# Second attention: maxima of block pairs from a difference and one block

## The chip, the cores and the metric

One core of one Trainium2 chip runs the kernel. The metric is device time in microseconds (us) of one execution, the median of the runs; lower is better. The engines are TensorE (PE), VectorE (DVE), ScalarE (ACT), GpSimd (POOL) and SyncE (SP), which here only issues transfers.

## What is computed

The reference is a network of two layers, each an attention and a feed-forward part with a layer norm behind each. The change is in the second attention, over 2048 tokens and 16 heads of 8 columns:

```python
G = -(j[None, None, None, :] - P[..., None]) ** 2 * 2.0 / Z[..., None] ** 2
scores = jnp.einsum('bhqd,bhkd->bhqk', q, k) / jnp.sqrt(jnp.float32(D))
scores = scores + G
probs = jax.nn.softmax(scores, axis=-1)
ctx = jnp.einsum('bhqk,bhkd->bhqd', probs, v)
ctx = ctx.transpose(0, 2, 1, 3).reshape(ctx.shape[0], key_len, H * D)
return ctx @ wo + bo
```

`P` and `Z` depend on the query and its head, `j` is the key's index. The softmax needs a maximum per query and head, or something near it, so that the exp doesn't overflow.

## The kernel before

The kernel runs four blocks of code one after the other: first attention, first feed-forward with the projections of the second attention, second attention with the last feed-forward. The change touches the last but one (a few transfers) and the last.

**Tiles and layout.** Queries and keys of a head lie as rows of bf16 parts: `qrows` and `krows` hold 60 rows per head (products of parts, and the rows that make up G), once in partitions 0 to 59 and once in 64 to 123. `krows` holds the first half of the keys in the lower copy and the second half in the upper one. Rows 60 and 61 of `qrows` take the negated maximum in two parts. A product over 60 or 62 rows uses half of TensorE's rows, so two that lie on different halves can run beside each other.

**Units.** A unit is one group of 4 heads (`HG`) with one chunk of 512 queries: 16 units (`NU`). Each has two kinds of work. The *blocks* find the maximum: for each head and each 128 queries, four products of 128 queries by 512 keys (`max_block`, L1757) into one of three PSUM banks of `ps_r`, each reduced over its keys by VectorE (L1899) into a column of `maxpart`. Block `b` has `k = b % 4`; `j = k % 2` is the half of the rows, and `c = k // 2` the chunk within it. That is 64 blocks a unit, 1024 in all. The *turns* do the attention itself: 8 turns a unit (`TU`), 128 in all, each with four heads. For one head TensorE makes two products of 128 keys by 512 queries into `ps_e` (`scores`, L1785), ScalarE takes the exp of both in one instruction (L1716), and TensorE multiplies the result with the values into `ps_o` (`pv`, L1795), for the turn before, in two halves of four heads.

**Order.** `plan()` writes it out. Before the first turn stand all 64 blocks of unit 0 and 8 of unit 1 (`BEFORE`), with four groups of small weight products among them (`weight_step`); ScalarE copies their results out. Then each turn carries 8 blocks, a unit and 8 blocks ahead (`blocks_of`), turns 0 to 118. The banks rotate: a block's product waits until the operation three places earlier in the order has been read out (`s_bf`). The PE loop of a turn:

```python
for hh in range(HG):
    scores(turn, hh)
    for op in rest[:1]:
        ring(op)
    if hh % 2 == late and turn > 0:
        pv(turn - 1, hh // 2)
    for op in rest[1:2]:
        ring(op)
    rest = rest[2:]
```

`late` is true in the second turn of a unit. `scores` waits until the exp of two heads before is done, `pv` until the exps of its turn are. Once a unit, VectorE makes the unit's maxima from `maxpart` (`split_max`, L1885 to L1891), TensorE transposes them (`mt`, L1769), VectorE copies them out (L1903), and SP sends them into rows 60 and 61 of `qrows` (`place_max`, L1638); the first `scores` of the next unit waits for that. Also once a unit, ScalarE copies `ps_o` out (L1723), TensorE transposes it (`fin`, L1774) and VectorE scales it (L1910, L1912). The last 9 turns have no blocks.

GpSimd adds a bias at the start of this part and then waits for the end. SP's queue loads the rows of the units ahead.

## Time and profile before

| | us |
|---|---|
| median of 3 runs (1779.0 to 1783.94) | 1779.66 |
| the profiled execution | 1781.96 |
| its span | 1780.2 |
| VectorE busy in the span | 1313.4 (74%) |
| TensorE busy (matmuls) | 1620.0 (91%) |
| ScalarE busy | 983.8 (55%) |
| GpSimd busy | 719.3 (40%) |
| reduces of blocks (L1899), 1024 | 634.4, 0.682 each |
| exps of the second attention (L1716), 512 | 504.8, 1.023 each |

The profile is of one execution. Busy times are sums of instruction spans; neighbours on one engine overlap by some 0.1 us, so a span is longer than the step from one to the next. In the timeline, rows merge neighbours of one kind: start, length of the whole row, engine, line, operation, out and in, count, and in brackets how long the engine had been idle before and what ended that. TensorE's granted clock (PEclk) is in parts of its full 2.4 GHz.

### The profile page before, as it was taken

The page shows a single profiled execution, that of the slowest core. Times are in us where ns is not written, and L with a number is a line of the kernel's source. Part 1 is how long each engine was busy: PE and PEld are TensorE (multiplying, and loading weights), DVE is VectorE, ACT ScalarE, POOL GpSimd, SP SyncE. Part 2 cuts the span into 40 slices and gives each one's busy share as a digit, 9 for nine tenths or more (in the row PEclk, how much of TensorE's full clock was granted, in tenths as well). Part 3 has the DMA queues.
Part 4 walks back from the last instruction along what each step waited for, and adds up shares of the span by engine and source line. Part 5 has one row for each costly group of instructions (what it writes and reads, how often), then busy time and mean ns, then how long its engine had stood idle before and what let it go on. Part 6 is the DMA issues. An engine that isn't in the chain of part 4 may idle for free. (4 is left out here: it accounts for less than half of the span.)

```text
span 1780.2 us, 28289 instructions
## 1 busy us (share of the span) xinstructions
PE 1620.0 (91%) x10680; PEld 477.6 (27%) x10680; DVE 1313.4 (74%) x2616; ACT 983.8 (55%) x1168; POOL 719.3 (40%) x462
## 2 busy tenths in 40 slices
PE   7899999999999999995988579999999999999995
PEld 3232333333332323222444211111111111111122
DVE  6767576666667575723555589999999999999964
ACT  2444545544545544442545306777777777777774
POOL 4577887878787878895222110000000000000012
PEclk8999999999999999996999758999999999999998
DMA  5100000000000000001012430111211121111000
GB/s 113 37 8 13 14 13 8 13 14 7 19 8 19 8 13 14 13 13 26 8 36 58 128 68 1 24 24 24 46 30 31 30 39 24 24 24 24 2 2 24
DMA packets 76217, 46.42 MB, mean 26 GB/s; under 512 B 22158, under 2 KB 74930, under 8 KB 76082
## 3 DMA queue, kind: packets, MB, share of 16 engines
q1 hardware_dynamic: 74738, 43.38, 11.4%
q8 instruction: 84, 1.38, 0.3%
q10 hardware_dynamic: 1344, 1.25, 0.2%
q14 instruction: 51, 0.42, 0.1%
HBM read 25.66 MB, written 9.31 MB: 20 GB/s over the span
## 5 line engine op out<-in xcount | busy, mean ns | idle before, releaser
L1899 DVE TENSOR_REDUCE maxpart<-ps_r 128x1 f32<-128x512 f32 x1024 | 634.4, 682 | 24.8 <-PE ps_r L1757 23.1
L1716 ACT ACTIVATE probs<-ps_e 128x1024 f32<-128x1024 f32 x512 | 504.8, 1023 | 193.1 <-PE ps_e L1785 187.9
L369 POOL TENSOR_TENSOR acc<-acc,probs 128x1024 f32<-128x1024 f32 (+3 forms) x256 | 503.2, 1965 | 77.6 <-ACT probs L422 56.1
L422 ACT ACTIVATE probs<-ps_e 128x1024 f32<-128x1024 f32 (+1 forms) x320 | 285.7, 901 | 371.0 <-PE ps_e L591 124.9
L1757 PE MATMUL ps_r<-krows,qrows 60*128 60x512 bf16 x1024 | 346.8, 402 | 50.5 <-DVE maxpart L1899 17.9
L608 PE MATMUL ps_o<-probs,v 128*64 128x512 f32 (+3 forms) x1280 | 307.6, 559 | 0.2 <-ACT pv_raw L429 0.2
L1681 POOL TENSOR_TENSOR rstd<-veps,power 128x4 f32<-128x4 f32 x8 | 8.1, 1012 | 698.5 <-DVE veps L1949 698.5
L698 DVE TENSOR_REDUCE maxpart<-ps_x 128x2 f32<-128x1024 f32 x192 | 234.5, 1221 | 74.7 <-PE ps_x L516 74.7
L1785 PE MATMUL ps_e<-qrows,krows 62*128 62x512 bf16 x1024 | 278.6, 386 | 2.3 <-ACT probs L1716 0.9
L1795 PE MATMUL ps_o<-probs,v 128*9 128x512 f32 x2048 | 269.5, 598 | 12.4 <-ACT probs L1716 12.3
L1757 PEld LDWEIGHTS ps_r<-krows,qrows 60*128 60x128 bf16 x1024 | 79.9, 94 | 468.2 <-DVE maxpart L1899 352.6
L701 DVE CUSTOM_DVE_ANT_0 masked<-ps_x,later 128x128 f32<-128x128 f32 (+3 forms) x256 | 114.9, 486 | 61.1 <-PE ps_x L516 60.0
L516 PE MATMUL ps_x<-k_hi,q_hi 64*128 64x512 f16 (+3 forms) x640 | 113.5, 351 | 21.0 <-DVE maxpart L698 17.3
L573 PE MATMUL ps_e<-q_hi,k_hi 64*128 64x512 f16 (+3 forms) x640 | 116.0, 359 | 0.4 <-ACT probs L422 0.3
L573 PE MATMUL ps_e<-q_lo,k_hi 64*128 64x512 f16 (+3 forms) x640 | 112.8, 349 | 0.0
L573 PE MATMUL ps_e<-q_hi,k_lo 64*128 64x512 f16 (+3 forms) x640 | 112.7, 349 | 0.0
L364 POOL TENSOR_TENSOR acc<-probs 128x1024 f32<-128x1024 f32 x32 | 75.2, 2351 | 79.6 <-ACT probs L422 79.6
L608 PEld LDWEIGHTS ps_o<-probs,v 128*64 128x64 f32 x1280 | 63.7, 135 | 87.0 <-issue 76.2
L780 DVE TENSOR_TENSOR ps_e<-ps_e,ahead 128x256 f32<-128x256 f32 (+1 forms) x128 | 55.5, 443 | 25.6 <-PE ps_e L573 16.2
L573 PEld LDWEIGHTS ps_e<-q_hi,k_hi 64*128 64x128 f16 x640 | 30.8, 93 | 159.1 <-issue 106.1
L1785 PEld LDWEIGHTS ps_e<-qrows,krows 62*128 62x128 bf16 x1024 | 58.6, 94 | 30.2 <-ACT probs L1716 11.8
L591 PE MATMUL ps_e<-mrow,negone 2*128 2x512 bf16 (+3 forms) x640 | 60.2, 356 | 0.0
(305 smaller groups left out, 1396.1 us busy)
## 6 DMA issues: line engine op xcount, KB each, us to landing
qrows<-q_rows SPq DMA_DIRECT2D x64, 192.0 KB
rbc<-rden SPq DMA_DIRECT2D x128, 64.0 KB, 2.1
q_rows<-parts_q SPq DMA_DIRECT2D x24, 128.0 KB, 2.3
k_rows<-parts_k SPq DMA_DIRECT2D x24, 128.0 KB, 2.3
krows<-k_rows SPq DMA_DIRECT2D x16, 192.0 KB, 5.4
w_rows<-parts_w SPq DMA_DIRECT2D x6, 256.0 KB, 2.6
qrows<-a_rows SPq DMA_DIRECT2D x64, 24.0 KB
qrows<-w_rows SPq DMA_DIRECT2D x64, 24.0 KB
```

Of the source, the lines that this page charges most:

```text
L369: pool.tensor_tensor(acc[:, u % 2, :, o:], acc[:, u % 2, :, o:], probs[:, turn % RING, :, o:], ALU.add)\
L422: act.activation(probs[:, turn % RING, :, o:], ps_e[:, turn % 2, :, o:], ACT.Exp, scale=1.0 / math.sqrt(D0))\
L516: mm = pe.matmul(ps_x[:, h, 0:w], hi["q"][rows, p % 2, (4 * qc + t) * P:(4 * qc + t + 1) * P], hi["k"][rows, p % 2, c * QC:c * QC + w], st ...
L573: mm = pe.matmul(out[:, h, o:], k_part["k"][rows, p % 2, keys], q_part["q"][rows, p % 2, queries], start=n == 0 and turn % 2 == 0, stop=n ...
L608: mm = pe.matmul(ps_o[D0 * h:D0 * h + D0, o:], v[:, p % 2, kt, D0 * h:D0 * h + D0], probs[:, turn % RING, h, o:], start=kt == 0, stop=kt = ...
L698: dve.reduce_max(maxpart[:, u % 2, :, t, c:c + 1], ps_x[:, :, 0:w], AX.X).then_inc(s_xf, 1)
L701: ins = dve.tensor_tensor_reduce(out=masked[:, h, 0:w], in0=ps_x[:, h, 0:w], in1=later[:, QC - w:QC], scale=1.0, scalar=-3e38, op0=ALU.add ...
L1716: act.activation(probs[:, HG * (turn % 2) + hh], ps_e[:, e % 2], ACT.Exp).then_inc(s_ex, 1)
L1757: return pe.matmul(out, qrows[64 * j:64 * j + R_M, u % 3, c, hh, t * P:(t + 1) * P], krows[64 * j:64 * j + R_M, u // NQ % 2, hh, c * KB:(c ...
L1785: mm = pe.matmul(ps_e[:, e % 2, j], krows[64 * j:64 * j + R_END, u // NQ % 2, hh, at * P:(at + 1) * P], qrows[64 * j:64 * j + R_END, u % 3 ...
L1795: mm = pe.matmul(ps_o[32 * hh:32 * hh + D1 + 1, :], v1[:, TU * j + at, HG * (u // NQ) + hh, :], probs[:, HG * (turn % 2) + hh, j, :], star ...
L1899: dve.reduce_max(maxpart[:, at:at + 1], ps_r[:, k, :], AX.X).then_inc(s_bf[k], 1)
```

## The change

For a pair of blocks `b` (even) and `b+1`, which have the same queries and the keys of the two halves, one product over 124 rows gives the difference of the two: its left side is both copies of the query rows, its right side the keys of the first block above and the *negated* keys of the second below (`nrows`). ScalarE takes the Relu of it (`over`). VectorE reads block `b+1` from its bank, adds `over` and takes the maximum in one instruction: the sum of `s1` and `relu(s0 - s1)` is the larger of the two. The first block isn't computed for itself. `DIFF` lists the pairs: in unit 0 and the 8 blocks ahead all but the first four pairs (32 pairs), then one pair in four, the first of each turn (119). In a turn the order of the 8 blocks becomes 0, 2, 3, 1, 4, 5, 6, 7.

`nrows` is filled by ScalarE (its negated half) and GpSimd (the copied half) for the first group, by GpSimd for the others. Rows 60 to 63 of `nrows` and `qrows` are set to zero by 8 transfers from `zrow`. `maxpart` is set to -3e38 first, so that the columns of the left-out blocks don't matter; PE waits for that memset too.

```diff
@@ stage before, SP @@
-            sp.wait_ge(s_cr, 5)
+            sp.wait_ge(s_cr, 6)
+            for row in range(R_M, 64):
+                sp.dma_start(qrows[row:row + 1].rearrange("a u c h (x n) -> a (u c h x) n", n=KB),
+                             zrow[0:1, :, :].to_broadcast([1, 3 * 2 * HG, KB])).then_inc(s_z, 16)
@@ stage before, DVE @@
+            dve.memset(zrow[0:1, :, :], 0.0).then_inc(s_cr, 1)
...
@@ blocks_of @@
-            return [("max", b) for b in range(first, min(first + LEAD, NU * BU))]
+            return [("max", first + n) for n in (0, 2, 3, 1, 4, 5, 6, 7) if first < NU * BU]
...
+        DIFF = {b: n for n, b in enumerate([b for b in range(2 * NC, BU + LEAD) if b % 2 == 0] +
+                                           [b for b in range(BU + LEAD, NU * BU) if b % (2 * NC) == 0])}
+        DIFF_OF = {b + 1: n for b, n in DIFF.items()}
+        RING_OF = {op[1]: op[2:] for op in ALL if op[0] == "max"}
+        JOINS = sorted(DIFF_OF)
@@ SP @@
+            for row in range(R_M, 64):
+                sp.dma_start(nrows[row:row + 1].rearrange("a b h (c n) -> a (b h c) n", n=KB),
+                             zrow[0:1, :, :].to_broadcast([1, 2 * HG * HALF // KB, KB])).then_inc(s_z, 16)
@@ POOL @@
+            def negate_k(g):
+                pool.wait_ge(s_k[g % 2], 16 * NQ * (g // 2 + 1))
+                rows = slice(64, 64 + R_M)
+                pool.tensor_scalar(nrows[rows, g % 2], krows[rows, g % 2], -1.0, None, ALU.mult).then_inc(s_neg, 1)
+                pool.wait_ge(s_neg, g + 1)
+
+            def copy_k(g):
+                pool.wait_ge(s_k[g % 2], 16 * NQ * (g // 2 + 1))
+                pool.tensor_copy(nrows[0:R_M, g % 2], krows[0:R_M, g % 2]).then_inc(s_cpy, 1)
+                pool.wait_ge(s_cpy, g + 1)
+
+            copy_k(0)
...
+            for g in range(1, NG):
+                negate_k(g)
+                copy_k(g)
@@ ACT @@
+            def positive(b):
+                n, (k, m) = DIFF[b], RING_OF[b]
+                act.wait_ge(s_bp[k], m + 1)
+                if n >= 2:
+                    k1, m1 = RING_OF[JOINS[n - 2]]
+                    act.wait_ge(s_bf[k1], m1 + 1)
+                act.activation(over[:, n % 2, :], ps_r[:, k, :], ACT.Relu).then_inc(s_bf[k], 1)
...
+            act.wait_ge(s_k[0], 16 * NQ)
+            rows = slice(64, 64 + R_M)
+            act.activation(nrows[rows, 0], krows[rows, 0], ACT.Copy, scale=-1.0).then_inc(s_neg, 1)
+            for n, op in enumerate(BEFORE):
+                if op[0] == "max" and op[1] in DIFF:
+                    positive(op[1])
+                if n in (8, 16, 24, 32):
+                    weights_out(n // 8 - 1)
             for turn in range(NU * TU):
                 u, at = divmod(turn, TU)
                 for hh in range(HG):
                     exps(HG * turn + hh)
+                    for op in TURNS[turn][2 * hh:2 * hh + 2]:
+                        if op[0] == "max" and op[1] in DIFF:
+                            positive(op[1])
@@ PE, max_block @@
+                if b in DIFF:
...
+                    return pe.matmul(out, qrows[0:64 + R_M, u % 3, c, hh, t * P:(t + 1) * P],
+                                     nrows[0:64 + R_M, u // NQ % 2, hh, c * KB:(c + 1) * KB], start=True, stop=True)
...
-            pe.wait_ge(s_cv, 2)
+            pe.wait_ge(s_cv, 3)
@@ DVE @@
             dve.memset(ps_o[:, :], 0.0).then_inc(s_cv, 1)
+            dve.memset(maxpart[:, :], -3e38).then_inc(s_cv, 1)
             dve.tensor_copy(identb[:, :], ident[:, :]).then_inc(s_cv, 1)
...
+                if kind == "max" and i in DIFF:
+                    return
                 dve.wait_ge(s_bp[k], m + 1)
-                if kind == "max":
+                if kind == "max" and i in DIFF_OF:
+                    at, n = i % (2 * BU), DIFF_OF[i]
...
+                    dve.tensor_tensor_reduce(out=larger[:, n % 2, :], in0=ps_r[:, k, :], in1=over[:, n % 2, :], scale=1.0, scalar=-3e38,
+                                             op0=ALU.add, op1=ALU.max, accum_out=maxpart[:, at:at + 1]).then_inc(s_bf[k], 1)
+                elif kind == "max":
```

What moves on TensorE in a steady turn. Before, from the block ahead of the first `pv` to the second `pv`, each row with the semaphore it waits for (`s_bf10` to `s_bf12` are the three banks of `ps_r`):

```order
L1757 MATMUL ps_r<-krows,qrows 128x512 [waits s_bf11]
L1795 MATMUL ps_o<-probs,v 9x512 [waits s_ex1]
L1795 MATMUL ps_o<-probs,v 9x512 x3
L1757 MATMUL ps_r<-krows,qrows 128x512 [waits s_bf12]
L1785 MATMUL ps_e<-qrows,krows 128x512 [waits s_ex1]
L1785 MATMUL ps_e<-qrows,krows 128x512
L1757 MATMUL ps_r<-krows,qrows 128x512 [waits s_bf10]
L1757 MATMUL ps_r<-krows,qrows 128x512 [waits s_bf11]
L1785 MATMUL ps_e<-qrows,krows 128x512 [waits s_ex1]
L1785 MATMUL ps_e<-qrows,krows 128x512
L1757 MATMUL ps_r<-krows,qrows 128x512 [waits s_bf12]
L1795 MATMUL ps_o<-probs,v 9x512 [waits s_ex1]
```

And with the change (L1823 is the product of the difference, L1825 a block, L1853 the scores, L1863 `pv`; the bank numbers are those of another turn, only their rotation matters):

```order
L1863 MATMUL ps_o<-probs,v 9x512 x3
L1825 MATMUL ps_r<-krows,qrows 128x512 [waits s_bf11]
L1853 MATMUL ps_e<-qrows,krows 128x512 [waits s_ex1]
L1853 MATMUL ps_e<-qrows,krows 128x512
L1825 MATMUL ps_r<-krows,qrows 128x512 [waits s_bf12]
L1825 MATMUL ps_r<-krows,qrows 128x512 [waits s_bf10]
L1853 MATMUL ps_e<-qrows,krows 128x512 [waits s_ex1]
L1853 MATMUL ps_e<-qrows,krows 128x512
L1825 MATMUL ps_r<-krows,qrows 128x512 [waits s_bf11]
L1863 MATMUL ps_o<-probs,v 9x512 [waits s_ex1]
L1863 MATMUL ps_o<-probs,v 9x512 x3
L1825 MATMUL ps_r<-krows,qrows 128x512 [waits s_bf12]
```

The product ahead of the first `pv` is now the difference. The block behind it still waits for one bank, and the block ahead of the second `pv` for the same bank again, as before.

What moves on ScalarE at the start of this part. Before, after the weight copies, it loads its table and starts on the exps:

```order
L1734 ACTIVATE w_t<-ps_e 128x128
L1734 ACTIVATE ua_t<-ps_e 50x128
L1734 ACTIVATE lu_t<-ps_e 4x50
L1734 ACTIVATE ld_t<-ps_e 100x4
L1737 ACTIVATE inner<-ps_e 4x128
L1737 ACTIVATE outer<-ps_e 50x128
L1737 ACTIVATE w_d<-ps_e 128x128
L1716 ACT_TABLE_LOAD
L1716 ACTIVATE probs<-ps_e 128x1024 x36
```

With the change, from behind the first four weight copies on (ahead of these rows stand the negation of the keys, one Relu and those four copies); L1774 is the Relu, L1785 a weight copy, L1753 the exp:

```order
L1774 ACTIVATE over<-ps_r 128x512 x4
L1785 ACTIVATE inner<-ps_e 4x128
L1774 ACTIVATE over<-ps_r 128x512 x4
L1785 ACTIVATE outer<-ps_e 50x128
L1774 ACTIVATE over<-ps_r 128x512 x4
L1785 ACTIVATE w_d<-ps_e 128x128
L1774 ACTIVATE over<-ps_r 128x512 x19
L1753 ACT_TABLE_LOAD
L1753 ACTIVATE probs<-ps_e 128x1024
L1774 ACTIVATE over<-ps_r 128x512
L1753 ACTIVATE probs<-ps_e 128x1024 x4
L1774 ACTIVATE over<-ps_r 128x512
```

The table load and the first exp now stand behind 32 Relus, and each turn's four exps have one Relu among them.

## Rows read from the trace of the kernel before

**Rows 1.** Windows: per stretch each engine's busy time (instructions), then PEclk, DMA share, GB/s.

```profile
1031.60:1071.00 39.40, 38.22 (x75) 7.50 (x75) 38.28 (x64) 2.82 (x8) 4.90 (x5) 0.50 0.27 50
1076.00:1084.50 8.50, 8.50 (x34) 1.42 (x34) 7.86 (x14) 6.14 (x6) 0.00 (x0) 0.50 0.01 2
...
1172.67:1215.25 42.58, 39.72 (x263) 7.93 (x261) 40.77 (x71) 31.94 (x33) 0.00 (x0) 1.00 0.12 25
```

**Rows 2.** Timeline of one steady turn, from PV1 to the next PV1.

```profile
1188.70 1.05 PE L1795 MATMUL ps_o<-probs,v 128*9 128x512 f32 x8 [0.16 <-ACT probs L1716]
...
1189.68 0.39 PE L1757 MATMUL ps_r<-krows,qrows 60*128 60x512 bf16 x1
1189.68 0.60 PE L1785 MATMUL ps_e<-qrows,krows 62*128 62x512 bf16 x2
...
1190.10 4.95 DVE L1899 TENSOR_REDUCE maxpart<-ps_r 128x1 f32<-128x512 f32 x8 [0.21 <-PE ps_r L1757]
...
1190.32 1.94 ACT L1716 ACTIVATE probs<-ps_e 128x1024 f32<-128x1024 f32 x2 [0.76 <-PE ps_e L1785]
...
1190.85 0.39 PE L1757 MATMUL ps_r<-krows,qrows 60*128 60x512 bf16 x1
...
1191.17 1.04 PE L1795 MATMUL ps_o<-probs,v 128*9 128x512 f32 x8
...
1192.79 1.94 ACT L1716 ACTIVATE probs<-ps_e 128x1024 f32<-128x1024 f32 x2 [0.53 <-PE ps_e L1785]
...
1193.86 1.05 PE L1795 MATMUL ps_o<-probs,v 128*9 128x512 f32 x8 [0.16 <-ACT probs L1716]
```

**Rows 3.** Timeline of DVE in the first attention; last row from the groups by shape.

```profile
768.53 0.69 DVE L701 CUSTOM_DVE_ANT_0 masked<-ps_x,later 128x512 f32<-128x512 f32 x1 [1.08 <-PE ps_x L516]
769.15 0.08 DVE L701 DVE_READ_ACCUMULATOR2_ANT maxpart<- 128x1 f32 x1
769.15 0.69 DVE L701 CUSTOM_DVE_ANT_0 masked<-ps_x,later 128x512 f32<-128x512 f32 x1
...
L1723 ACT ACTIVATE pv_raw<-ps_o 128x512 f32<-128x512 f32 x16 | 9.5, 592 | 2.0 <-PE ps_o L1795 2.0
```

**Rows 4.** Timeline around the end of a unit: PV1 of four turns, and the maximum's way.

```profile
1172.67 1.04 PE L1795 MATMUL ps_o<-probs,v 128*9 128x512 f32 x8
...
1199.03 1.05 PE L1795 MATMUL ps_o<-probs,v 128*9 128x512 f32 x8 [0.16 <-ACT probs L1716]
...
1201.60 0.20 DVE L1903 COPY maxrow<-ps_r 64x128 bf16<-64x128 bf16 x1
...
1204.61 0.39 PE L1785 MATMUL ps_e<-qrows,krows 62*128 62x512 bf16 x2
...
1205.14 1.04 PE L1795 MATMUL ps_o<-probs,v 128*9 128x512 f32 x8
...
1215.25 1.05 PE L1795 MATMUL ps_o<-probs,v 128*9 128x512 f32 x8
```

**Rows 5.** Timeline: a GpSimd cast in the stage before, then the first unit.

```profile
1002.90 0.61 POOL L1071 CAST parts_q<-qs 128x512 bf16<-128x512 f32 x1 [7.97 <-DVE qs L1413]
...
1031.66 1.01 PE L1757 MATMUL ps_r<-krows,qrows 60*128 60x512 bf16 x3 [17.28 <-DMA qrows<-w_rows]
...
1032.28 4.28 DVE L1899 TENSOR_REDUCE maxpart<-ps_r 128x1 f32<-128x512 f32 x7 [0.96 <-PE ps_r L1757]
...
1041.83 0.59 PE L1810 MATMUL ps_e<-end_da,ld_t 100*4 100x128 f32 x2
...
1052.40 1.28 ACT L1716 ACT_TABLE_LOAD   x1
...
1072.14 0.29 PE L1769 MATMUL ps_r<-identb,maxhl 128*64 128x128 bf16 x1 [1.38 <-DVE maxhl L1891]
...
1075.91 0.66 PE L1785 MATMUL ps_e<-qrows,krows 62*128 62x512 bf16 x2
...
1076.61 1.02 ACT L1716 ACTIVATE probs<-ps_e 128x1024 f32<-128x1024 f32 x1 [22.93 <-PE ps_e L1785]
```

More of the change, by code:

```diff
@@ L823, in build @@
     qrows = l1.enter_context(nc.sbuf_tensor("qrows", [P, 3, 2, HG, QC], BF16))
+    zrow = l1.enter_context(nc.sbuf_tensor("zrow", [1, 1, KB], BF16))
+    s_z = l1.enter_context(nc.semaphore("s_z"))
     s_q = [l1.enter_context(nc.semaphore(f"s_q{b}")) for b in range(3)]
@@ L1523, in build @@
         rowmax = sb("rowmax1", [P, HG * 4], F32)
+        nrows = sb("nrows", [P, 2, HG, HALF], BF16)
+        over = sb("over", [P, 2, QC], F32)
+        larger = sb("larger", [P, 2, QC], BF16)
         maxhl = sb("maxhl1", [P, 2, 2, HG * 4], BF16)
@@ L1552, in build @@
         s_bf = [sem(f"s_bf1{k}") for k in range(3)]
+        s_neg = sem("s_neg1")
+        s_cpy = sem("s_cpy1")
         s_rm = sem("s_rm1")
@@ L1729, in copy_step, with weights_out @@
                                ACT.Copy).then_inc(s_bf[k], 1)
-            for n, (dst, rows, cols) in enumerate(((w_t, P, DM), (ua_t, UD, P), (lu_t, RANK, UD), (ld_t, DD, RANK))):
-                act.wait_ge(s_lp, n + 1)
-                act.activation(dst[:, :], ps_e[0:rows, n // 2, n % 2, 0:cols], ACT.Copy).then_inc(s_lc, 1)
-            for n, (dst, rows) in enumerate(((inner, RANK), (outer, UD), (w_d, P))):
+            def positive(b):
[5 more added lines that the diff above has]
+                act.activation(over[:, n % 2, :], ps_r[:, k, :], ACT.Relu).then_inc(s_bf[k], 1)
+            def weights_out(step):
+                if step == 0:
+                    for n, (dst, rows, cols) in enumerate(((w_t, P, DM), (ua_t, UD, P), (lu_t, RANK, UD), (ld_t, DD, RANK))):
+                        act.wait_ge(s_lp, n + 1)
+                        act.activation(dst[:, :], ps_e[0:rows, n // 2, n % 2, 0:cols], ACT.Copy).then_inc(s_lc, 1)
+                    return
+                n = step - 1
+                dst, rows = ((inner, RANK), (outer, UD), (w_d, P))[n]
                 act.wait_ge(s_lp, 5 + n)
                 act.activation(dst[:, :], ps_e[0:rows, n // 2, n % 2, P:2 * P], ACT.Copy).then_inc(s_lc, 1)
+            act.wait_ge(s_k[0], 16 * NQ)
[6 more added lines that the diff above has]
+                    weights_out(n // 8 - 1)
             for turn in range(NU * TU):
@@ L1756, in max_block @@
                     pe.wait_ge(s_k[u // NQ % 2], 16 * NQ * (u // NQ // 2 + 1))
+                if b in DIFF:
+                    if b == 2 * NC:
+                        pe.wait_ge(s_z, 16 * 2 * (64 - R_M))
+                    if b == 2 * NC or b % (NQ * BU) == 0:
+                        pe.wait_ge(s_neg, u // NQ + 1)
+                        pe.wait_ge(s_cpy, u // NQ + 1)
+                    return pe.matmul(out, qrows[0:64 + R_M, u % 3, c, hh, t * P:(t + 1) * P],
+                                     nrows[0:64 + R_M, u // NQ % 2, hh, c * KB:(c + 1) * KB], start=True, stop=True)
                 return pe.matmul(out, qrows[64 * j:64 * j + R_M, u % 3, c, hh, t * P:(t + 1) * P],
@@ L1968, in normalize @@
                     ins.then_inc(s_no, 1)
+            dve.wait_ge(s_cv, 3)
             done = 0
```

10 lines of the change are left out of this document (9 added, 1 removed).

## The prediction

> **What bounds the kernel now.** I read the views in this order. The windows [rows 1] first: the first unit of the second attention (64 blocks, 1032 to 1071 us) runs with VectorE busy nearly all the time and TensorE's granted clock at 0.50 (the 1.2 GHz level), and a later unit takes 42.58 us with VectorE busy for 40.77 of them and ScalarE for 31.94. By shares, VectorE looks like the bound. The timeline of one turn [rows 2] says otherwise. I call the block products M0 to M7, the score products S, the first and second half of the probs-times-v products PV1 and PV2. From PV1 at 1188.70 the chain is: M1 starts 0.98 later (1189.68), VectorE starts its reduce 0.42 after that (1190.10), M4 needs the bank which that reduce empties and starts 0.75 later (1190.85), PV2 0.32 later (1191.17), then the last head's S and its exp, whose start is 1.62 after PV2 (1192.79), and the next PV1 waits for that exp: 1.07 (1193.86). The sum is 5.16, which is the distance of the two PV1. VectorE's eight reduces (4.95) lie beside it, with 0.21 idle. So one reduce is on the chain, the seven others are not: a steady turn is a loop of latencies through three engines, only 0.21 longer than VectorE's own work.
>
> **The change in the steady turn.** Per turn it removes one reduce on VectorE and gives ScalarE a Relu of 128x512. The joined maximum is a two-input operation with an accumulator; the same one in the first attention took 0.69, the read of its accumulator lay beside the next operation, and the next one started 0.62 after it [rows 3]. Reduces start (4.95-0.68)/7 = 0.61 apart [rows 2]. So the join costs what one reduce costs, and VectorE falls from 4.95 to about 4.33 a turn. The Relu has no row; the copy of the same shape took 0.592 [rows 3], half an exp's step would be 0.46. I take 0.59. It comes after the turn's first exp, where ScalarE sat idle 0.76 [rows 2], so it fits and no exp moves.
>
> What I look for is whether the loop above loses a link. It doesn't. The order of the blocks is now D0 (the difference), M2, M3, B1 (the partner), M4. With three banks in rotation M4 needs the bank of M2, the product right behind PV1, as it needed that of M1 before. The links 0.98, 0.42, 0.75, 0.32, 1.62, 1.07 all stay, and the turn stays at 5.16. VectorE only idles more, 0.83 instead of 0.21.
>
> D0 is new work on TensorE: it fills all the rows, so it can't run beside a score product on the other half, as M0 did. A half-height product takes one slot of 0.215 (two S in 0.60, one alone 0.39 [rows 2]). VectorE takes M2 1.40 after PV1 (0.98+0.42), then M3, B1, M4 and M5 at 0.615 each, so M5 starts at 3.87, D0's bank is free 0.75 later, at 4.62, and the next PV1 stands at 5.16: it may take 0.54 up to PV1. From M4 to PV2, which is also a product and a change of tile form, took 0.32 [rows 2]. I take 0.32 for D0, 0.42 if a change ahead of it costs the same 0.1 as the one behind it. Both are under 0.54, so in a steady turn it costs nothing; its cover is the wait for the exp. The Trainium skill ("TensorEngine Tiling (Array Packing)", Key Properties) says that changing the tiling mode drains TensorE. By it every D0 has a drain on both sides; by the row alone one drain of 0.1 stands in the 0.32. The sum is the same either way until the two together pass 0.54.
>
> **Turns that are not steady**, once a unit. (a) The last turn: its first PV1 to the next unit's is 6.11 instead of 5.16 [rows 4], since the transposed maximum is copied at 1201.60 behind two reduces, and the next unit's S waits for the transfer until 1204.61, 3.01 later. One of the reduces in front is gone (M0's), so copy and transfer come 0.55 earlier, and S at 5.03 after PV1 instead of 5.58. Late next is D0's bank: PV2 at 2.55, M4's reduce at 3.95, M5's at 4.57, D0 at 5.32, PV1 at 5.68 with 0.36 for D0. Gain 0.43. (b) From the first to the third turn, 10.11 [rows 4]. PV1 and PV2 of the second turn come one head later, so in the third there is no exp to wait for, and D0's slot and drain (0.32) stand in the open: 10.43, loss 0.32. (c) From 1172.67 to 1199.03 are five turns, 26.36; four steady ones leave 5.72 for the one that transposes the context; the reordered blocks move nothing there that I can see. Net gain 0.1 a unit, 1.5 for 15 units; bounds -7 and +7 (half a us a unit either way, the size of (a) and (b)).
>
> **The first unit.** Eight plain blocks as before, so D8 starts near 1032.28 + 5x0.60 + 0.73 = 1036.0, plus 0.1 for the extra memset that the products wait for [rows 5]. The negated and copied keys must be there: 4096 elements are 3.7 us on ScalarE at an exp's rate (0.92 per 1024, [rows 2]) and 4.9 on GpSimd at that of the cast of 512 in 0.61 [rows 5]; started at about 1030.6 they end by 1035.5. The eight extra transfers of zeros are on SP's queue ahead of loads needed 35 us later, and in the stage before ahead of ones waited for much later: nothing. GpSimd's bias adds move back by 5 us and are waited for at the end only; its six later passes over the keys lie in idle time.
>
> Then pairs. At half clock a product takes 0.43, twice the slot, and I add 0.1 for each change between half and full height: D and B together 1.06. The other loop is D, 0.62 to the Relu (as 1031.66 to 1032.28, [rows 5]), 0.59, 0.04, join 0.69, 0.05 to the product after next: 2.0 for two pairs. So 1.06 per pair, TensorE now the bound, against 1.20 for two reduces. 28 pairs are 29.7; the four groups of weight products (0.59 for one [rows 5], put at 0.6 each) had been beside VectorE's work and are now on the path: 2.4. D64 starts at 1068.2, the transposed maximum 1.9 later (join, three small operations) at 1070.1, against 1072.14: gain 2.0. The first exp was at 1076.61; its table load of 1.28 lay in idle time and now stands behind the last Relu [rows 5]: D70 near 1073.0, +0.62 +0.59 +1.28 = 1075.5, gain 1.1, with 0.3 won back in the first turn: 1.4. Bounds: 6 lost if a pair takes 1.3, 5 more gained if it takes 0.90.
>
> **Sum.** 1.4 + 1.5 = 2.9. Against the profiled execution (span 1780.2, time 1781.96, so 1.8 around it): span 1777.3, time 1779.1. That execution is 2.3 above the median of the three runs, 1779.66; against the median I forecast 1776.7. A measurement of this kernel can tell about 0.3%, 5.3 us, from no change, so this is no difference.
>
> **Rivals.** (A) Faster: the clock rises in the first unit. TensorE's rows show 0.50 both while one product ran per 0.60 and in the first turn with four per 1.20 [rows 1], rising only after the first PV. Pairs put a full-height product into each 1.06, more work than the first unit had but no more than that turn had. If it rises after a quarter of the pairs, a pair takes 0.90 (the 2.0 loop with products at full clock): 24x0.16 = 3.8, and about 2 from the first turns: 1771. The rows of the first turn speak against, the fuller engine for: 0.2. The Trainium skill ("TensorE: Matmul & The Clock Gate", What's actually happening) has the array throttled by default and activity release it; by that rule a fuller engine may rise, and the first turn's rows agree with it only in part.
> (B) Much faster: VectorE was the bound after all, and a turn gets shorter by the reduce that left. The busy share speaks for it, the chain of [rows 2] against. The floor then is that chain without the bank wait: M4 four slots behind M2, 0.98+4x0.215 = 1.84 after PV1 instead of 2.15, so 4.85; 119 turns x 0.31 = 37, less 3 more: 1740. Chance 0.07.
> (C) Slower: D0 delays PV1. It decides at 0.54 from D0's start to PV1. If weight load and drains ahead of and behind a full-height product come to 0.3 to 0.5 more than its slot, each turn is longer by 0 to 0.18; at 0.15 it is 119x0.15 = 18, less 3: 1795. For it: it is one change of form more per turn, and no row shows such a product there. Against: the 0.32 measured. Chance 0.15. The drains of the page on tiling are this mechanism.
> (D) The first unit's pairs take 1.3 or more: (1.3-1.06)x32 = 8, less 3: 1784. Chance 0.05.
>
> **Numbers.** Forecast 0.53, own range 1772 to 1781. Faster by over 0.3%: A 0.2, B 0.07, and 0.08 of the forecast where the units gain more: 0.35. Slower: C 0.15, D 0.04: 0.19. The rest, 0.46, within. The range 1767 to 1787 takes in A, the forecast, D and the mild end of C.
>
> **What would show it.** Right: PV1 to PV1 5.16 in steady turns with VectorE idle 0.8; Relu about 0.59 and join 0.69; 6.1 becoming 5.7 at a unit's end, 10.1 becoming 10.4; pairs 1.06 apart at clock 0.50; the first exp near 1075.5. Wrong: a steady turn of other than 5.16 (below: B, above with D0 just ahead of PV1: C), or the clock above 0.50 before 1070 (A).

## The result and the profile after

| | us | ratio to the kernel before, 95% interval |
|---|---|---|
| before, median of 20 runs | 1780.68 | |
| after, median of 20 runs | 1784.81 | 1.0023 [1.0014, 1.0032] |
| after, the profiled execution | 1782.89 | |
| its span | 1780.9 | |

The change makes the kernel 4.1 us slower, 0.23%. The forecast was a gain of 2.9. The time lies in the stated range (1767 to 1787) but outside the forecast's own (1772 to 1781), and the change is below the 5.3 us that the prediction took as the limit of one measurement; with 20 runs of each it is told from nothing all the same, and its sign is the other one.

Of the turns the profile says what was forecast. Groups of instructions (line, engine, operation, count, then busy us and mean ns, then idle time before and what ended it); reduces of the same shape were 1024 before:

```profile
L1979 DVE TENSOR_REDUCE maxpart<-ps_r 128x1 f32<-128x512 f32 x722 | 460.1, 684 | 85.5 <-PE ps_r L1825 85.5
...
L1975 DVE CUSTOM_DVE_ANT_0 larger<-ps_r,over 128x512 bf16<-128x512 f32 x151 | 103.2, 684 | 23.8 <-PE ps_r L1825 23.3
...
L1774 ACT ACTIVATE over<-ps_r 128x512 f32<-128x512 f32 x151 | 90.7, 601 | 22.4 <-PE ps_r L1823 22.4
```

151 joins and 151 Relus stand in place of 302 reduces. VectorE is busy for 1231.7 us instead of 1313.4, ScalarE for 1061.5 instead of 983.8. A steady turn from its timeline, one turn ahead of the one in [rows 2]:

```profile
1181.52 0.39 PE L1823 MATMUL ps_r<-nrows,qrows 124*128 124x512 bf16 x1
1182.07 1.04 PE L1863 MATMUL ps_o<-probs,v 128*9 128x512 f32 x8 [0.16 <-ACT probs L1753]
1182.81 0.60 ACT L1774 ACTIVATE over<-ps_r 128x512 f32<-128x512 f32 x1
...
1183.47 1.29 DVE L1979 TENSOR_REDUCE maxpart<-ps_r 128x1 f32<-128x512 f32 x2 [0.81 <-PE ps_r L1825]
...
1184.22 0.39 PE L1825 MATMUL ps_r<-krows,qrows 60*128 60x512 bf16 x1
1184.53 1.05 PE L1863 MATMUL ps_o<-probs,v 128*9 128x512 f32 x8
1184.68 0.68 DVE L1975 CUSTOM_DVE_ANT_0 larger<-ps_r,over 128x512 bf16<-128x512 f32 x1
...
1186.68 0.39 PE L1823 MATMUL ps_r<-nrows,qrows 124*128 124x512 bf16 x1
1187.23 0.62 PE L1863 MATMUL ps_o<-probs,v 128*9 128x512 f32 x4 [0.16 <-ACT probs L1753]
```

PV1 to PV1 is 1187.23 - 1182.07 = 5.16, as before. VectorE starts its first reduce 1.40 after PV1 and has been idle 0.81 by then, not 0.21. The difference product D0 starts 0.55 ahead of the next PV1, and PV1 is released by the exp, not by D0. VectorE gave up 0.6 a turn and nothing moved: it was not the bound.

What did move stands at the entry of the second attention. The executions reach it at different times (1030.7 in the profile of before, 1027.9 in that of after; in the executions of the experiments from 1027.3 to 1034.2), so from here on I align the traces at VectorE's first memset of this stage. The entry after:

```profile
1027.71 3.61 ACT L1789 ACTIVATE nrows<-krows 60x4096 bf16<-60x4096 bf16 x1 [8.58 <-PEq L862]
1027.71 3.59 POOL L1691 COPY nrows<-krows 60x4096 bf16<-60x4096 bf16 x1 [23.84 <-POOLq L862]
1027.88 0.48 DVE L1943 MEMSET ps_o<- 128x512 f32 x1 [7.23 <-PEq L862]
1028.38 0.17 DVE L1944 MEMSET maxpart<- 128x128 f32 x1
1028.46 2.93 DVE L1945 CAST identb<-ident 128x128 bf16<-128x128 f32 x1
...
1031.44 1.03 PE L1825 MATMUL ps_r<-krows,qrows 60*128 60x512 bf16 x3 [20.03 <-DVE identb L1945]
```

and before, where the first product came 0.95 after the memset [rows 5]:

```profile
1030.71 0.48 DVE L1875 MEMSET ps_o<- 128x512 f32 x1 [7.09 <-PEq L860]
1031.11 0.21 DVE L1876 CAST identb<-ident 128x128 bf16<-128x128 f32 x1
```

The cast of the identity matrix takes 2.93 instead of 0.21. It ends at 1031.39, 0.09 after GpSimd's copy of the keys has ended (1027.71 + 3.59), and TensorE's first product waits for it: 3.56 after the memset instead of 0.95, so 2.6 are lost. None of the tiles that these three operations write is read by that product: `ps_o` is first used by `pv`, `identb` by `mt`, `maxpart` by VectorE itself. The wait asks for more than the product needs; whether moving it to the first use would do as well as the experiments below was not run.

The Trainium skill ("SBUF — State Buffer", Who interferes with whom) says that GpSimd has no port of its own into this memory but VectorE's second pair, that a VectorE copy or cast can take both pairs, and that the one which comes second is then blocked for the whole instruction of the other. The two numbers, 2.93 and 0.09, agree with it.

Behind that, the first unit ran at the forecast pace (windows, columns as in [rows 1], then its timeline):

```profile
1032.00:1071.00 39.00, 37.35 (x78) 7.95 (x75) 25.39 (x69) 18.48 (x36) 19.08 (x7) 0.50 0.29 49
```

```profile
1066.01 0.61 PE L1823 MATMUL ps_r<-nrows,qrows 124*128 124x512 bf16 x1
...
1067.09 0.61 PE L1823 MATMUL ps_r<-nrows,qrows 124*128 124x512 bf16 x1
...
1074.18 1.28 ACT L1753 ACT_TABLE_LOAD   x1
...
1075.47 1.02 ACT L1753 ACTIVATE probs<-ps_e 128x1024 f32<-128x1024 f32 x1
```

A pair takes 1.08 and the granted clock stays at 0.50, though TensorE is busy for 37.35 of 39.00 us (whole spans count, 0.61 for one product), now in part with full-height products.

The third piece is in the units. I took the start of every PV1 and PV2 in both traces. Per unit there are 16 distances, and 12 of them are the same to 0.02. The other four, as means over 14 units:

| distance (the D0 or the blocks of that place) | before | after | forecast |
|---|---|---|---|
| PV2 to PV1, issued in the third turn (D0 in the open) | 1.52 | 1.84 | +0.32 |
| PV1 to PV2, in the same turn (the context's transposition between) | 2.64 | 2.85 | 0 |
| PV1 to PV2, issued in the last turn (one reduce fewer ahead) | 2.96 | 2.53 | -0.43 for these two |
| PV2 to PV1, issued in the next unit's first turn (D0 behind S) | 3.21 | 3.29 | |

In sum a unit is 0.18 longer, not 0.1 shorter. The context's turn in both timelines, TensorE's rows, before and after:

```profile
1217.36 0.39 PE L1757 MATMUL ps_r<-krows,qrows 60*128 60x512 bf16 x1
1217.36 0.60 PE L1785 MATMUL ps_e<-qrows,krows 62*128 62x512 bf16 x2
1217.59 0.38 PE L1757 MATMUL ps_r<-krows,qrows 60*128 60x512 bf16 x1
1217.90 0.62 PE L1795 MATMUL ps_o<-probs,v 128*9 128x512 f32 x4
```

```profile
1215.84 0.39 PE L1825 MATMUL ps_r<-krows,qrows 60*128 60x512 bf16 x1
1215.84 0.60 PE L1853 MATMUL ps_e<-qrows,krows 62*128 62x512 bf16 x2
1216.28 0.38 PE L1825 MATMUL ps_r<-krows,qrows 60*128 60x512 bf16 x1
1216.59 0.62 PE L1863 MATMUL ps_o<-probs,v 128*9 128x512 f32 x4
```

The second block starts 0.23 after the first before, 0.44 after it now, and PV2 with it. Before, the two blocks around the score products were M2 (lower half of the rows) and M3 (upper); now they are M3 and B1, both upper, and one of the two score products is on that half too.

**Theory.** The loss has three parts: the blocked cast at the entry (2.6), D0 where no exp covers it (0.32, and 0.1 behind S), and the order of the blocks in the context's turn (0.21). Rivals: the start is bound by ScalarE's negation or the copy itself and not by the cast, or it is the negation that holds the cast; the drift along the units comes from GpSimd's later passes or from the join; VectorE's work does bound the turn in some way.

### The profile page after: what moved, and what is told of

Read it like the earlier page. It is cut to its first block and busy times, and to the rows that moved or that the text cites. A ratio compares the mean times of both kernels' runs of the same rounds, so it can differ in the third digit from the quotient of the medians.

```text
span 1780.9 us, 28771 instructions
## 1 busy us (share of the span) xinstructions
PE 1619.8 (91%) x10680; PEld 478.5 (27%) x10680; DVE 1231.7 (69%) x2618; ACT 1061.5 (60%) x1320; POOL 764.9 (43%) x469
## 5 line engine op out<-in xcount | busy, mean ns | idle before, releaser
L1753 ACT ACTIVATE probs<-ps_e 128x1024 f32<-128x1024 f32 x512 | 503.9, 1026 | 116.8 <-PE ps_e L1853 113.4
L1979 DVE TENSOR_REDUCE maxpart<-ps_r 128x1 f32<-128x512 f32 x722 | 460.1, 684 | 85.5 <-PE ps_r L1825 85.5
L1825 PE MATMUL ps_r<-krows,qrows 60*128 60x512 bf16 x873 | 287.2, 395 | 43.9 <-DVE identb L1945 20.0
L1863 PE MATMUL ps_o<-probs,v 128*9 128x512 f32 x2048 | 269.0, 598 | 12.2 <-ACT probs L1753 12.1
L1853 PE MATMUL ps_e<-qrows,krows 62*128 62x512 bf16 x1024 | 276.7, 385 | 3.1 <-DMA qrows<-maxrow 1.0
L1686 POOL TENSOR_SCALAR nrows<-krows 60x4096 bf16<-60x4096 bf16 x3 | 31.6, 10547 | 346.0 <-DMA krows<-k_rows 345.9
L1825 PEld LDWEIGHTS ps_r<-krows,qrows 60*128 60x128 bf16 x873 | 67.7, 94 | 395.8 <-DVE maxpart L1979 215.8
L1975 DVE CUSTOM_DVE_ANT_0 larger<-ps_r,over 128x512 bf16<-128x512 f32 x151 | 103.2, 684 | 23.8 <-PE ps_r L1825 23.3
L1774 ACT ACTIVATE over<-ps_r 128x512 f32<-128x512 f32 x151 | 90.7, 601 | 22.4 <-PE ps_r L1823 22.4
```

What stands on the lines that cost most here:

```text
L1753: act.activation(probs[:, HG * (turn % 2) + hh], ps_e[:, e % 2], ACT.Exp).then_inc(s_ex, 1)
L1825: return pe.matmul(out, qrows[64 * j:64 * j + R_M, u % 3, c, hh, t * P:(t + 1) * P], krows[64 * j:64 * j + R_M, u // NQ % 2, hh, c * KB:(c ...
L1853: mm = pe.matmul(ps_e[:, e % 2, j], krows[64 * j:64 * j + R_END, u // NQ % 2, hh, at * P:(at + 1) * P], qrows[64 * j:64 * j + R_END, u % 3 ...
L1863: mm = pe.matmul(ps_o[32 * hh:32 * hh + D1 + 1, :], v1[:, TU * j + at, HG * (u // NQ) + hh, :], probs[:, HG * (turn % 2) + hh, j, :], star ...
L1975: dve.tensor_tensor_reduce(out=larger[:, n % 2, :], in0=ps_r[:, k, :], in1=over[:, n % 2, :], scale=1.0, scalar=-3e38, op0=ALU.add, op1=AL ...
L1979: dve.reduce_max(maxpart[:, at:at + 1], ps_r[:, k, :], AX.X).then_inc(s_bf[k], 1)
```

## The experiments

Each ran beside the kernel before. The ratio is the recorded one; that of the two medians can differ from it by 0.001. The last column is aligned at the memset, from the profiles: how much later the last PV1 stands than in the profile of before (726.57 after the memset there).

| run | ratio | 95% interval | last PV1, us |
|---|---|---|---|
| the change | 1.0023 | [1.0014, 1.0032] | +3.6 |
| cast ahead of the copy | 0.9998 | [0.9987, 1.0008] | +0.4 |
| the same, pairs in the turns only | 1.0016 | [1.0006, 1.0027] | +2.5 |
| the same, pairs in the first unit only | 0.9998 | [0.9990, 1.0007] | -1.1 |
| the same, third turn plain | 0.9969 | [0.9957, 0.9980] | -6.8 |
| the same, blocks 0, 3, 2, 1 | 0.9983 | [0.9972, 0.9994] | -2.5 |
| before, order alone | 1.0026 | [1.0013, 1.0038] | +3.8 |
| cast ahead, PV2 ahead everywhere | 0.9981 | [0.9970, 0.9993] | -3.4 |
| cast ahead, pair in the last turn only | 0.9955 | [0.9942, 0.9968] | -7.9 |
| PV2 ahead in turns 5 to 7, pairs in 5 to 8 | 0.9937 | [0.9919, 0.9955] | -10.3 |
| PV2 ahead in turns 5 to 7, pair in 8 | 0.9945 | [0.9928, 0.9962] | -12.2 |
| change, reduce in place of the cast | 0.9998 | [0.9985, 1.0010] | -0.3 |
| PV2 ahead in turns 5 and 6, pairs in 5 to 8 | 0.9921 | [0.9909, 0.9934] | -13.2 |

The last column compares single executions, and two places in it vary from one to the next. From PV1 to PV2 of the first turn it is 3.53 before, 2.73 in the change, 2.47 with the cast ahead and 3.75 with the pair in the last turn only; in that turn the granted clock rises (before: PV1 at 1082.65, 0.50 up to 1084.50, 0.84 in the next 2.5 us; after: PV1 at 1081.52, 0.50 up to 1082.00, 0.98 in the next 2.0 us). And the last of the 15 unit ends (the last two distances of the table above) takes 4.32 in three of these traces (blocks 0, 3, 2, 1; PV2 ahead with the pair in turn 8; the reduce) and 5.55 to 5.74 in the others. So a difference of about 1 us in that column says nothing; the distances between PV1 and PV2, which repeat unit for unit, do.

**The cast ahead of the copy.**

```diff
+            pool.wait_ge(s_cv, 3)
             copy_k(0)
```

> One edit: GpSimd starts its copy of the first key group only after VectorE's three small operations at the second attention's entry (two memsets, cast of the identity matrix). Theory P (the cast of 0.2 us takes 2.9 because it shares something with the GpSimd copy that runs beside it, and TensorE's first product waits for the cast): cast back to 0.2 to 0.3, first product 1.1 to 1.5 after the entry instead of 3.7, first PV1 51.2 after the entry instead of 53.8, time 2.6 less than the change: kernel before + 0.9 (+0.3 to +1.8). Rival Q (the start is bound by the negation of 3.6 us on ScalarE and by the copy's end, the cast only hides in front of them): first pair not earlier, time as the change, kernel before + 3.5 to + 4.

Measured: medians of 1780.99 and 1779.49, ratio 0.9998, which tells nothing from the kernel before; the last PV1 stands 0.4 later than there, 3.2 earlier than in the change. Entry of this kernel:

```profile
1029.60 3.61 ACT L1790 ACTIVATE nrows<-krows 60x4096 bf16<-60x4096 bf16 x1 [8.58 <-PEq L862]
...
1030.35 0.16 DVE L1946 CAST identb<-ident 128x128 bf16<-128x128 f32 x1
1030.58 3.59 POOL L1691 COPY nrows<-krows 60x4096 bf16<-60x4096 bf16 x1 [24.66 <-DVE identb L1946]
...
1030.76 1.01 PE L1826 MATMUL ps_r<-krows,qrows 60*128 60x512 bf16 x3 [17.46 <-DMA qrows<-w_rows]
```

The first product comes 0.99 after the memset (1029.77), the first PV1 at 50.86, against 53.64 in the change and 51.94 before. The copy starts 1.0 later against the memset and delays nothing: the first D0 comes 5.42 after the memset, in the change 8.01. The rival is out. The cast takes 0.16 here although ScalarE's negation runs beside it as before, so it is the GpSimd copy that held it.

**A reduce in place of the cast**, the copy left where the change has it. A maximum over groups of one element gives the same values:

```diff
-            dve.tensor_copy(identb[:, :], ident[:, :]).then_inc(s_cv, 1)
+            dve.reduce_max(identb[:, :], ident[:, :].rearrange("p (n c) -> p n c", c=1), AX.X).then_inc(s_cv, 1)
```

> The changed kernel with one edit: the identity matrix goes to bf16 by a maximum over groups of one element in place of the copy, beside the same GpSimd copy, which starts at the entry as in the change. Theory K (only the form in which VectorE copies fp32 to bf16 takes the port that it shares with GpSimd; a reduce reads through its own): the operation takes 0.2 to 0.35 and doesn't wait, first product 1.2 to 1.5 after the entry, time as with the cast edit: kernel before - 0.4 (-1.5 to +0.8). Rival J (any VectorE operation that reads this memory waits for the GpSimd copy): 2.9 as before, kernel before + 4.

```profile
1028.18 3.59 POOL L1691 COPY nrows<-krows 60x4096 bf16<-60x4096 bf16 x1 [23.39 <-POOLq L862]
...
1028.92 0.23 DVE L1945 TENSOR_REDUCE identb<-ident 128x128 bf16<-128x128 f32 x1
...
1029.35 1.01 PE L1825 MATMUL ps_r<-krows,qrows 60*128 60x512 bf16 x3 [17.26 <-DMA qrows<-w_rows]
```

The same bytes, read and written by the same engine beside the same copy: 0.23 instead of 2.93, and the copy still takes 3.59. It is the form of the instruction that is blocked, not VectorE's access as such. The same section of the Trainium skill says that a reduce never contends on this chip; the row agrees.

**Pairs in the turns only, pairs in the first unit only** (both with the cast ahead).

```diff
-        DIFF = {b: n for n, b in enumerate([b for b in range(2 * NC, BU + LEAD) if b % 2 == 0] +
-                                           [b for b in range(BU + LEAD, NU * BU) if b % (2 * NC) == 0])}
+        DIFF = {b: n for n, b in enumerate([b for b in range(BU + LEAD, NU * BU) if b % (2 * NC) == 0])}
```

(and TensorE's waits for the filled `nrows` move to the first pair that is left).

> The cast edit of the run above, and no pairs in the first unit; the pair of each later turn stays. Theory U (the units lose by the pair and by its order: +0.33 where the difference product stands in the open, +0.2 in the turn that transposes the context, -0.53 at the unit's end, and 0.1 to 0.2 from the next turns, 0.15 a unit): kernel before + 2.3 (+1.5 to +3.2), with the turn-to-turn distances of the change. Rival V (the drift along the units came from the GpSimd passes over the keys or from the transfers and not from the turns' order): distances of PV1 drift only near those passes; kernel before + 0 to + 1.

```diff
-            return [("max", first + n) for n in (0, 2, 3, 1, 4, 5, 6, 7) if first < NU * BU]
+            return [("max", first + n) for n in (0, 1, 2, 3, 4, 5, 6, 7) if first < NU * BU]
...
-            for g in range(1, NG):
-                negate_k(g)
-                copy_k(g)
```

(and only the first list in `DIFF`).

> The cast edit, pairs in the first unit alone; the later turns have the natural order, no pair, and GpSimd makes no passes over the later key groups. Theory P and U: first unit gains its 1.1 to 1.6, turns as in the kernel before: kernel before - 1.5 (-2.3 to -0.7). Rival (the first unit's pairs gain nothing once the start is mended, since TensorE is its bound at 1.2 GHz): 0.

Turns only: 1.0016, which is 2.9 us, and the four distances of the table above are those of the change (1.84 and 2.85 in the third turn), although the first unit is that of the kernel before. First unit only: the first PV1 at 50.30 (1.6 earlier), the third PV at 55.57 (1.4 earlier), and the 16 distances of a unit as before. Of that gain of 1.4 the ratio, 0.9998 [0.9990, 1.0007], shows nothing by itself; it can't, at 0.08%. In this run GpSimd's later passes are missing too, in the other they are there; the distances that moved stand in every unit, while three pairs of passes make no such pattern. The run with the pair in the last turn only (below) has all the passes, and the distances of its other turns are those of the kernel before: the passes cost nothing that shows.

**Third turn plain.** The turn with the open D0 and the transposition goes back to plain blocks in natural order:

```diff
+            order = (0, 1, 2, 3, 4, 5, 6, 7) if turn % TU == 2 else (0, 2, 3, 1, 4, 5, 6, 7)
+            return [("max", first + n) for n in order if first < NU * BU]
```

(and `DIFF` leaves out the pairs of these turns).

> The cast edit, and the third turn of each unit (the one with the context's transposition, whose difference product stands in the open) goes back to plain blocks in natural order; all other turns keep their pair. Theory U: both losses (0.33 and 0.20) come from this one turn and leave with it, 15 units x 0.53 = 8 less than the run with the cast edit alone: kernel before - 7 (-8.5 to -5.5). Rival W (only the open difference product, 0.33, belongs to that turn; the 0.2 comes back elsewhere, or the gain of 0.5 at the unit's end shrinks): kernel before - 4 (-5 to -2.5).

1773.80, ratio 0.9969 (5.5 us): both losses leave with this one turn (7.2 by the aligned profiles), and the gain at the unit's end stays.

**Order alone, and another order with the pair.**

```diff
-            return [("max", b) for b in range(first, min(first + LEAD, NU * BU))]
+            return [("max", first + n) for n in (0, 2, 3, 1, 4, 5, 6, 7) if first < NU * BU]
```

> The kernel before with nothing but the turns' order of blocks 0, 2, 3, 1, 4 .. 7; no difference product, no Relu, no join. Theory H: the 0.21 of the context's turn is the order's and is seen here too, with the 10.1 of the first to the third turn otherwise as before: kernel before + 3 (+2 to +3.5). Rival R (it is the join's or the Relu's): kernel before + 0.

```diff
-            return [("max", first + n) for n in (0, 2, 3, 1, 4, 5, 6, 7) if first < NU * BU]
+            return [("max", first + n) for n in (0, 3, 2, 1, 4, 5, 6, 7) if first < NU * BU]
```

> As the run with the cast edit alone, but the turns take their blocks as 0, 3, 2, 1, 4 .. 7 instead of 0, 2, 3, 1, 4 .. 7 (same pair, same number of products). Theory H (in the turn that transposes the context, the product ahead of PV2 is the second in a row on the upper half of the array's rows, behind a score product on that half, and so starts 0.21 later; with halves in turn it doesn't): PV1 to PV2 of that turn back from 2.85 to 2.65, 15 x 0.21 = 3 less than the run with the cast edit: kernel before - 3.4 (-4.5 to -2.5). Rival R (it is the bank of the block behind the transposition, or VectorE's join, that comes 0.2 later whatever the half): distances unchanged, kernel before - 0.4.

The order alone makes the kernel before slower by 1.0026, with 2.85 in the context's turn and 1.52 ahead of it. With 0, 3, 2, 1 the pair is the same and the distance is 2.64 again in all 14 units; 1.84 stays. Its rows, with M2 (lower) and B1 (upper) around the score products:

```profile
1220.05 0.39 PE L1826 MATMUL ps_r<-krows,qrows 60*128 60x512 bf16 x1
1220.06 0.60 PE L1854 MATMUL ps_e<-qrows,krows 62*128 62x512 bf16 x2
1220.29 0.38 PE L1826 MATMUL ps_r<-krows,qrows 60*128 60x512 bf16 x1
```

0.24 apart. Neither Relu nor join has to do with the 0.21; which half a block lies on has.

**PV2 ahead of M4.** The forecast held that the turn is a chain through M4's bank. If so, taking PV2 out from behind M4 must move it:

```diff
+                    ahead = turn > 0 and hh == 2 + late
+                    if ahead:
+                        pv(turn - 1, 1)
                     for op in rest[:1]:
                         ring(op)
-                    if hh % 2 == late and turn > 0:
-                        pv(turn - 1, hh // 2)
+                    if turn > 0 and hh == late:
+                        pv(turn - 1, 0)
```

> The cast edit, and TensorE issues PV2 ahead of M4 instead of behind it, so that PV2 no longer waits for the bank that the first reduce behind PV1 empties. Theory N (the turn is a net of nearly equal loops: then M4 and M5 follow PV2 by 0.98, the reduce of M5 starts 2.05 + 0.98 + 0.42 + 0.62 = 4.07 after PV1, the difference product needs that bank 0.75 later and PV1 follows 0.32 behind it: 5.14): PV2 2.0 to 2.1 after PV1 instead of 2.47, turn 5.1 to 5.2, time within 3 of the run with the cast edit. Rival L (the loop through M4's bank is the only one near 5.16, then the last exp binds at 2.05 + 0.98 + 0.64 + 1.07 = 4.74): turn 4.75 to 4.85, 35 to 50 less. Rival B (VectorE's work was the bound of the turn, the chain only followed it): turn near 4.4, 90 less.

```profile
1182.71 1.05 PE L1864 MATMUL ps_o<-probs,v 128*9 128x512 f32 x8
...
1184.67 1.05 PE L1864 MATMUL ps_o<-probs,v 128*9 128x512 f32 x8
...
1186.07 2.48 DVE L1983 TENSOR_REDUCE maxpart<-ps_r 128x1 f32<-128x512 f32 x4
...
1186.82 0.39 PE L1826 MATMUL ps_r<-krows,qrows 60*128 60x512 bf16 x1 [0.35 <-DVE maxpart L1983]
...
1187.42 0.39 PE L1824 MATMUL ps_r<-nrows,qrows 124*128 124x512 bf16 x1
1187.74 1.05 PE L1864 MATMUL ps_o<-probs,v 128*9 128x512 f32 x8
```

PV2 comes at 1.96 instead of 2.46, and the turn is 5.03: of the 0.50 the next loop takes back 0.37. M7 waits for the bank that the reduce of M4 (1186.07) empties; D0 at 1187.42 is 0.60 behind it, and also 0.73 behind the start of M5's reduce, so which of the two holds D0 can't be told here. Rivals L (4.75 to 4.85) and B (near 4.4) are out. Theory N, nearly equal loops, is what is left, but its numbers missed: PV2 came 0.1 earlier, the turn is 5.03 and not 5.1 to 5.2, and the time is below the run with the cast edit by 3.0 us by the ratios and 3.7 by the aligned profiles, at the edge of its 3. Two other turns give some of it back: against the run with the cast ahead, the context's turn goes from 5.92 to 6.32 and the one at the unit's end from 5.81 to 6.19, while the shortest falls from 4.31 to 3.79 (PV1 to PV1, means over 14 units). In sum a unit is 0.22 shorter, and the ratio 0.9981.

**Pair in the last turn only.**

```diff
+            order = (0, 2, 3, 1, 4, 5, 6, 7) if turn % TU == TU - 1 else (0, 1, 2, 3, 4, 5, 6, 7)
```

(and `DIFF` limited to the same turns).

> The cast edit, pairs in the first unit and in the last turn of each unit alone; the seven other turns of a unit are plain and in natural order. Theory U (only the last turn's pair gains, 0.53 a unit; the first turn's difference product costs 0.12 there, the third turn's 0.33 and its order 0.21, the others' nothing): kernel before - 1.6 - 14 x 0.5 = - 8.5 (-10 to -6.5), that is 1 to 3 less than with plain blocks in the third turn only. Rival (the less VectorE has to do in all turns is what lets the last turn be shorter): kernel before - 3 or more.

1770.66, ratio 0.9955: 8.0 us faster than the kernel before (the medians are 10.0 apart), with 14 of the 119 pairs in the turns left. PV1 to PV2 in the last turn is 2.46 against 2.96 before; the other distances are as before, and from S to PV1 it is 0.53 again, since no D0 stands between them.

**PV2 ahead where it pays.** Three kernels, all with the cast ahead; order and `DIFF` are limited to the turns that the texts name:

```diff
+                    ahead = turn % TU in (4, 5, 6) and hh == 2
+                    if ahead:
+                        pv(turn - 1, 1)
                     for op in rest[:1]:
                         ring(op)
-                    if hh % 2 == late and turn > 0:
+                    if hh % 2 == late and turn > 0 and not ahead:
```

> The cast edit; pairs in the first unit and in the fifth to eighth turn of each unit (natural order and plain blocks in the first to fourth); PV2 ahead of M4 in the fifth to seventh turn. Theory: the steady turns with PV2 ahead take 5.02, as they did where every turn had PV2 ahead, instead of 5.16, the rest as with the pair in the last turn alone: 15 x 3 x 0.14 = 6.3 less than that, kernel before - 14 (-16 to -11). Rival (what one turn gains is given back in the last one, which took 5.76 instead of 5.24 with PV2 ahead everywhere): kernel before - 8.

> As the run with PV2 ahead in the fifth to seventh turn, but those turns have plain blocks (eight reduces on VectorE, 4.95); the pair stays in the first unit and in the last turn. Theory S (the second loop, not VectorE, sets the turn here too; the pair in a steady turn buys nothing): 5.0 to 5.05 a turn, kernel before - 13 or - 14. Rival T (with PV2 ahead VectorE's eight reduces and their waits become the bound, and this is where the pair pays): 5.1 to 5.2 a turn, kernel before - 8 to - 10.

With pairs in those turns: 0.9937, about 3 less than the pair in the last turn alone, where 6.3 was expected. The rival is half right: the turns take 5.02, and the last one gives back 0.22 (2.69 instead of 2.46). Plain blocks in those turns: 0.9945, and 5.01 to 5.08 a turn. By the turn Theory S is nearer (Rival T had 5.1 to 5.2), but the time, 9.8 us below the kernel before, is the one that T gave (8 to 10); the interval, 6.8 to 12.8, ends just short of the 13 of S. What a pair buys here can be read in the traces: PV1 to PV2 is 1.95 instead of 2.01 in the sixth and seventh turn, 1.7 us over 15 units. The ratios, whose intervals overlap, do not show it. The last variant has `(4, 5)` in place of `(4, 5, 6)`:

> As the run with PV2 ahead in the fifth to seventh turn and pairs in the fifth to eighth, but PV2 ahead in the fifth and sixth only. In that run each turn with PV2 ahead began 0.52 earlier with PV2 and gave 0.38 back, and the eighth turn gave back 0.22 more. Theory X (the 0.22 is the price of having PV2 ahead in the turn before the last one): 2 x 0.14 = 0.28 a unit instead of 0.17, kernel before - 12.5 (-14 to -11), PV1 to PV2 of the eighth turn's list position back to 2.47. Rival (the 0.22 comes from the pairs or from any turn with PV2 ahead): 2.69 there, kernel before - 10.

1766.24 against 1780.00, ratio 0.9921: 14.1 us faster than the kernel before, the lowest of these, though its interval overlaps those of the two others. The distance in the last turn is 2.52, as Theory X had it.

## Why the prediction was wrong, point by point

- **Steady turn (5.16, VectorE idle 0.8, Relu 0.59, join 0.69 in a step of 0.62):** right in each number: 5.16, 0.81, 0.60, 0.68 in 0.60. The chain was read rightly, and it is why the 0.6 less work on VectorE a turn bought nothing there.
- **D0 covered in a steady turn:** right, and rival C with it wrong: 0.55 from D0 to PV1, which the exp releases. D0 to PV1 in the open is 0.32 in every such place.
- **The first unit's pace:** right: 1.08 a pair against 1.06, first PV1 1.1 earlier once the cast is out of the way, clock 0.50. Two numbers owe something to luck. The first exp at 1075.47 is the 1075.5 of the forecast only because this execution reached the entry 2.8 earlier; from the memset it is 1.7 later than before. And the gain of the first unit and turn, 1.7 instead of 1.4 (the third PV is 1.2 later, with 2.6 of the entry and 0.3 of the first open D0 in it), has a part from the first turn that changes with when the clock rises. Rivals A and D are wrong, although D's 1784 is the time that was measured: its pairs of 1.3 did not come. The Trainium skill ("TensorE: Matmul & The Clock Gate", What's actually happening) has activity release the throttle; a TensorE that is busy for 96% of the first unit, with the taller products, was not released in it.
- **"Plus 0.1 for the extra memset that the products wait for": this step failed.** I had looked at what the new entry work costs the engine that does it (the copy 4.9, measured 3.59) and when it must end. I had not looked at what runs beside it: the products wait for three VectorE operations, and the third is a cast that GpSimd's copy blocks. Price 2.6 instead of 0.1, shown by both entry runs.
- **(c) "the reordered blocks move nothing there that I can see": this step failed too.** They move which half of the array two neighbouring blocks lie on. Price 0.21 in 14 turns, 3.0 in sum, shown by the order alone and by the order 0, 3, 2, 1.
- **(b) The open D0:** right, 0.32 in each unit.
- **(a) The unit's end: mechanism right, the term over 15 units mis-sized.** 6.11 to 5.68 forecast, 5.74 measured there; the means give -0.43 + 0.08. The copy of the maximum comes 0.56 earlier (2.01 after PV1 instead of 2.57, in 13 of 14 units; forecast 0.55). From S to PV1 it is 0.64 instead of 0.53. From the copy to S it is 3.14 instead of 3.09 as means of 14, each between 2.99 and 3.36; the forecast took the 3.01 of one. I had named D0's bank as late next. It is S, which waits for the transfer of the maximum; D0 and its change of form stand behind it, in the timeline after:

```profile
1197.56 1.04 PE L1863 MATMUL ps_o<-probs,v 128*9 128x512 f32 x8 [0.15 <-ACT probs L1753]
...
1202.65 0.39 PE L1853 MATMUL ps_e<-qrows,krows 62*128 62x512 bf16 x2
1202.98 0.39 PE L1823 MATMUL ps_r<-nrows,qrows 124*128 124x512 bf16 x1
1203.30 1.05 PE L1863 MATMUL ps_o<-probs,v 128*9 128x512 f32 x8
```

S is at 5.09 (forecast 5.03), D0 0.33 behind it and PV1 0.32 behind D0. The half-height M0 stood 0.22 behind S at this place (1204.61 and 1204.83, PV1 at 1205.14), so the change of form ahead of D0 costs 0.11 and the one behind it nothing beyond what stood ahead of PV1 already. The Trainium skill ("TensorEngine Tiling (Array Packing)", Key Properties) names such a drain without a figure; the 0.11 agrees with it.
- **The sum:** -2.9 + 2.6 + 3.0 = +2.7; the aligned traces show +3.6. The rest of 0.9 is the unit's end: 15 x 0.43 = 6.5 was forecast, 5.3 came (0.38 on average in 14, nothing in the last), less the 0.3 that the first unit and turn gained beyond their 1.4. The medians show +4.1, and their interval, 2.5 to 5.7, holds the 3.6.
- **Rival B (VectorE the bound):** wrong in the turns; with PV2 ahead pairs or plain blocks differ by 0.06 in two turns and by nothing that the ratios show.

The forecast treated the net of a unit, +0.43 - 0.32, as two large terms that nearly cancel, with bounds of 7. Those bounds held the units' loss (2.3 from the third PV to the last PV1); the entry was outside them, as its cost was put at 0.1 without its cover being named.

## What to carry to other kernels

When a loop is a chain through several engines, as here, taking work off the busiest of them can change nothing in the steady part (0.6 of 5.16 here); look at the few unsteady places per unit, where the same edit can gain (here 0.43 at a unit's end) and lose (0.32 and 0.21 in the third turn), and apply it only where it gains. Work given to an idle engine still needs a look at what its neighbours run in the same microseconds: here 3.6 us of GpSimd copying held a 0.2 us cast on which the first product waited. And an order changed for one reason also changes which half of TensorE each product uses.
